# Ten expert tiles turned on VectorE and through DRAM, nine row buffers, and one early table of expert biases

## What is computed

```python
x = x + tanh(g_xattn) * attention(layernorm(x), ctx_1024, ...)   # 8 batches of 512 rows of 512
# the experts, over all 4096 rows at once:
xt = layernorm(x).reshape(4096, 512)
probs = softmax(xt @ router_w + router_b)
gate, idx = max(probs), argmax(probs)                  # one of 8 experts for each row
e_out = xt @ expert_w[idx] + expert_b[idx]
x = x + tanh(g_ffn) * gate * e_out
```

## Time and profile before

| | before |
|---|---|
| median of three runs | 1065.18 us (1064.52 to 1066.03) |
| the profiled execution | 1071.23 us, span of the trace 1069.5 us |
| TensorE busy, share of the span | 1057.6 us, 99% |
| TensorE weight loads | 864.1 us, 81% |
| VectorE busy | 790.9 us, 74% |
| ScalarE busy | 431.9 us, 40% |
| GpSimd busy | 214.8 us, 20% |
| DMA | 146.03 MB, mean 137 GB/s |

### The profile page before, as it was taken

The page is one execution under the profiler, slowest core; times in us unless marked ns, Lnnn a source line. Parts: engine busy times, 40 slices in busy tenths (PEclk is TensorE's granted clock), DMA queues, the critical chain, the costliest instruction groups (busy, mean ns, idle before and its releaser), DMA issues.

```text
span 1069.5 us, 16036 instructions
## 1 busy us (share of the span) xinstructions
PE 1057.6 (99%) x5119; PEld 864.1 (81%) x5119; DVE 790.9 (74%) x1634; ACT 431.9 (40%) x768; POOL 214.8 (20%) x319
## 2 busy tenths in 40 slices
PE   9999999999999999999999999999999999998998
PEld 7878887888788888888888888887888787886886
DVE  6886976777767876677768677866687677976665
ACT  6334623352325242533344234423352346532432
POOL 3000101130113001400140013101220112256664
PEclk9999999999999999999999999999999999998999
DMA  8337416431643254334354335325531754585542
GB/s 300 134 109 226 161 22 174 138 125 39 141 143 112 99 119 124 124 127 99 109 160 128 80 116 171 128 56 140 171 99 24 205 180 146 185 284 180 158 153 75
DMA packets 135468, 146.03 MB, mean 137 GB/s; under 512 B 25242, under 2 KB 87222, under 8 KB 135288
## 3 DMA queue, kind: packets, MB, share of 16 engines
q1 hardware_dynamic: 125248, 119.60, 38.3%
q0 software_dynamic: 7264, 19.20, 5.6%
q10 hardware_dynamic: 2904, 6.63, 1.8%
HBM read 101.30 MB, written 45.93 MB: 138 GB/s over the span
## 4 chain that ended last, share of the span: by engine, by line
PE 89%; DVE 4%; DMA 3%; issue 2%; SPq 1%; ACT 1%; another core or an unknown queue 0%; POOL 0%; DVEq 0%; ACTq 0%; POOLq 0%
PE mm L168 60%; PE u L1145 15%; PE u L168 9%; PE tr L168 2%; PE mm L2027 1%; DVE arena L1382 1%; DMA in_tile<-in_ctx 1%; DMA probs_by_keys<-pairs_as_f 1%; PE tr L1199 1%; DMA slot_as_f<-in_L_xattn_Wk_s 1%; DMA x_rows_early<-slot_as_f 0%; DMA slot_as_f<-in_x_by_blocks 0%; SPq L897 0%; PE tr L1189 0%; ACT probs L1259 0%
## 5 line engine op out<-in xcount | busy, mean ns | idle before, releaser
L168 PE MATMUL mm<-arena 128*128 128x512 f32 x1512 | 356.1, 390 | 0.8 <-DVE arena L1382 0.6
L168 PEld LDWEIGHTS mm<-arena 128*128 128x128 f32 x1512 | 282.5, 188 | 64.6 <-ACT probs L1259 4.1
L168 PE MATMUL mm<-arena,q_pair 128*128 128x512 f32 x768 | 184.1, 394 | 0.0
L1145 PE MATMUL u<-arena 128*128 128x512 f32 x768 | 182.9, 390 | 0.7 <-DVE arena L1382 0.7
L1145 PEld LDWEIGHTS u<-arena 128*128 128x128 f32 x768 | 143.4, 188 | 31.0 <-DVE arena L1382 1.5
L168 PEld LDWEIGHTS mm<-arena,q_pair 128*128 128x128 f32 x768 | 142.0, 188 | 29.4 <-issue 0.5
L1607 POOL TENSOR_SCALAR stats<-stats 128x1 f32<-128x1 f32 x28 | 11.3, 405 | 545.6 <-DVE stats L1521 545.0
L1259 ACT ACTIVATE probs<-mm,neg_top 128x512 f32<-128x512 f32 x64 | 44.2, 690 | 147.9 <-DVE neg_top L1405 147.9
L1252 ACT ACTIVATE arena<-mm 128x512 fp32r<-128x512 f32 x64 | 38.3, 598 | 136.0 <-PE mm L168 121.8
L1382 DVE TENSOR_TENSOR arena<-mm,arena 128x512 fp32r<-128x512 f32 x65 | 44.5, 684 | 65.8 <-ACT arena L1252 39.7
L168 PE MATMUL mm<-q_pair,arena 128*128 128x512 f32 x360 | 86.3, 389 | 0.0
(11 more groups left out here) (281 smaller groups left out, 1441.3 us busy)
## 6 DMA issues: line engine op xcount, KB each, us to landing
slot_as_f<-in_ctx_by_columns SPq DMA_DIRECT2D x8, 1024.0 KB
probs_by_keys<-slot_as_f SPq DMA_DIRECT2D x32, 256.0 KB, 4.1
pairs_as_f<-probs_by_keys SPq DMA_DIRECT2D x8, 1024.0 KB, 5.5
probs_by_keys<-pairs_as_f SPq DMA_DIRECT2D x32, 256.0 KB, 4.5
probs<-probs_by_keys SPq DMA_DIRECT2D x8, 1024.0 KB, 5.6
in_tile<-in_ctx SPq DMA_DIRECT2D x31, 256.0 KB
in_tile<-in_x SPq DMA_DIRECT2D x28, 256.0 KB
slot_as_f<-in_x_by_columns SPq DMA_DIRECT2D x7, 1024.0 KB, 7.0
```

Of the source, the lines that this page charges most:

```text
L168: last = pe.matmul(bank, lhsT(a, c), rhs(b, c), start=start and n == 0, stop=stop and n == C * len(PASSES) - 1)
L1145: last = pe.matmul(u_bank[m][:], v_pair[:, i % 2, a, tile(m)], pt_pair[:, i % 2, p], start=i == 0 and n == 0, stop=i == T - 1 and n == 2)
```

## The change

- Tiles 15, 17, 23, 25, and so on to 37 (TURNED) are no longer transposed by TensorE. ScalarE normalises such a tile in stage n - 6. VectorE transposes its 32 x 32 blocks in stage n - 5, SyncE stores the result to DRAM and in stage n - 4 loads it again in four parts that put the blocks in their places. `high` and `low` in stage n - 1 read the landed tile from SBUF.
- So that both ways give the same order of columns, ScalarE writes the normalised rows of the other tiles in a block order, and the expert weights are given in that order.
- There are nine row buffers from tile 12 on, and the step in which each row is gathered is given by `step_of_gather`.
- The table of all expert biases is loaded once, before T 0, to where the attention's first pair lay, and all tiles read it. The loads of single biases are gone.
- Rows 3, 4 and 5 are gathered when the gate is done (3 and 4 came earlier), and all four residual chunks are loaded then (the first came earlier).
- From T 1 on the steps of the last batch stand one T later in the list.
- Outputs have six buffers, and the wait for a free one stands in `add_bias`.

```diff
-ROWS, NORMED, PAIR, BIAS, BANK, OUT = 6, 3, 3, 5, 4, 5
-FROM_SLOT = 4
-BY_TABLE, LOAD_TABLE = 12, 6
+ROWS, PAIR, BANK, OUT = 9, 3, 4, 6
+SIX_ROWS = 12
+TURNED = (15, 17) + tuple(range(23, TILES, 2))
...
+    turned_dram = [nc.dram_tensor(f"turned_rows{i}", (P, H), F32, kind="Internal").ap() for i in range(2)]
...
-    s += steps("GC2") + load(22, 23) + steps("GC3") + load(24, 25, 26, 27) + steps("EL7") + gather(3, 4)
-    s += steps("RP0 GS0 TN0 XR0 GS1 TP0") + load(28, 29, 30, 31)
+    s += steps("GC2") + load(22, 23) + steps("GC3") + load(24, 25, 26, 27) + steps("EL7")
+    s += steps("RP0 GS0 TN0 GS1 TP0") + load(28, 29, 30, 31)
...
-    names = """GA5 T0 XR1 XR2 XR3 T1 M0 M1 MX0 MX1 BS0 T2 M2 M3 MX2 MX3 BS1 T3 LG0 LG1 BS2 T4 LG2 LG3 BS3 LR3 T5 RT0 IW0
-               T6 RK0 T7 RS0 TB3 T8 RS1 TB4 T9 RS2 T10 RS3 TB5 T11 TB6 T12 T13 LI0 T14"""
+    names = """GA3 GA4 GA5 T0 XR0 XR1 T1 XR2 XR3 T2 M0 M1 MX0 MX1 BS0 T3 M2 M3 MX2 MX3 BS1 T4 LG0 LG1 BS2 T5 LG2 LG3 BS3
+               LR3 T6 RT0 IW0 T7 RK0 T8 RS0 TB3 T9 RS1 TB4 T10 RS2 T11 RS3 TB5 T12 TB6 T13 LI0 T14"""
...
-        sp.wait_ge(x1_stats, 4 * (B - 1))
-        load_last_residual(0)
         for n in range(EARLY // LOADS):
             experts_run("IX", n)
+        sp.wait_ge(gc_mm, 1)
+        for of_last in range(E - 1, E + 1):
+            sp.wait_ge(ex_loaded[of_last], 16)
         experts_run("BIAS", 0)
         sp.wait_ge(g_mm, 4 * B)
-        for c in range(1, C):
+        for c in range(C):
             load_last_residual(c)
...
+    row = [k.in_tile[:, n] for n in range(3)] + [q[:, 4 * H + n * ROWX:4 * H + (n + 1) * ROWX] for n in range(3)]
+    table = c2s.rearrange("p (e d) -> p e d", e=E)
+    row += [slot[:, n * ROWX:(n + 1) * ROWX] for n in range(3)]
+    stage, landed = slot[:, 5 * H:6 * H], [slot[:, n * H:(n + 1) * H] for n in (6, 7)]
+
+    def row_no(n):
+        return n % 6 if n < SIX_ROWS else (n - SIX_ROWS + 6) % ROWS
...
             elif kind == "BIAS":
-                sp.wait_ge(experts_ready, 1)
-                load_bias(0)
+                sp.dma_start(c2s, expert_b.rearrange("e d -> (e d)").partition_broadcast(P)).then_inc(table_loaded, 16)
             elif kind == "T":
...
+                if i + 5 in TURNED:
+                    m = turned_no(i + 5)
+                    sp.wait_ge(turned, probs_turned_in_all + m + 1)
+                    sp.dma_start(turned_dram[m % 2], stage).then_inc(turned_kept, 16)
+                if i + 4 in TURNED:
+                    m = turned_no(i + 4)
+                    sp.wait_ge(turned_kept, turned_kept_in_all + 16 * (m + 1))
+                    if m > 1:
+                        sp.wait_ge(e_lo, TURNED[m - 2] + 1)
+                    if m > 0:
+                        sp.wait_ge(e_hi, TURNED[m - 1] + 1)
+                    for r in range(T):
+                        rows_of_chunk = turned_dram[m % 2].rearrange("(t i) (r n) -> r i t n", i=32, r=T)[r]
+                        sp.dma_start(landed[m % 2][32 * r:32 * r + 32].rearrange("i (t n) -> i t n", t=T),
+                                     rows_of_chunk).then_inc(e_landed, 16)
+                if FIRST_LATE <= i:
+                    for n in range(EARLY + LOADS + 2 * (i - FIRST_LATE), min(EARLY + LOADS + 2 * (i - FIRST_LATE) + 2, TILES)):
+                        load_idx(n)
...
             elif n == 3:
-                pool.wait_ge(attention.gc_mm, 1)
-            elif n == 5:
                 pool.wait_ge(attention.g_mm, 4 * B)
...
+        def step_of_gather(n):
+
+            if n < SIX_ROWS:
+                return n - 5
+            return max(n - 8, 15 + (n - EARLY) // 2) if n >= EARLY else max(n - 8, SIX_ROWS - 5)
...
             elif kind == "T":
-                if ROWS <= i + ROWS - 1 < TILES and i > 0:
-                    gather(i + ROWS - 1)
+                for n in range(6, TILES):
+                    if i == step_of_gather(n):
+                        gather(n)
                 scatter(i)
...
                 if i + 1 < TILES:
                     high(i + 1)
-                if i + 2 < TILES:
+                if i + 2 in by_pe:
                     normalise(i + 2)
+                if i + 6 in TURNED:
+                    normalise(i + 6)
...
+        def turn(n):
+            m = turned_no(n)
+            dve.wait_ge(e_normed, normed_in_order.index(n) + 1)
+            if m > 0:
+                dve.wait_ge(turned_kept, turned_kept_in_all + 16 * m)
+            dve.transpose(stage.rearrange("p (c j) -> p c j", j=32),
+                          normed_of(n).rearrange("p (c j) -> p c j", j=32)).then_inc(turned, 1)
...
                     low(i + 1)
                 add_bias(i)
+                if i + 5 in TURNED:
+                    turn(i + 5)
                 finish(i)
...
-                if i + 1 < TILES:
+                if i + 1 in by_pe:
                     transpose_rows(i + 1)
```

More of the change, by code:

```diff
@@ L607, in attention_part @@
     probs = sb("probs", [P, T, L])
+    with nc.sbuf_tensor("first_pair", [P, 2, C, P], F32R) as first_pair:
+        pass
     normed = sb("normed", [P, H])
@@ L1732, in experts_part @@
[L1732 to L1748, removed]
+    n_pair = [[attention.first_pair[:, a] for a in (HI, LO)]] + [[pair_in(attention.q_pair, n)[:, a] for a in (HI, LO)] for n in range(2)]
@@ new lines, in row_no, with users_of_row, row_is_loaded, turned_no @@
+    def row_no(n):
+        return n % 6 if n < SIX_ROWS else (n - SIX_ROWS + 6) % ROWS
+    def users_of_row(n):
+        return [m for m in range(n) if row_no(m) == row_no(n)]
+    def row_is_loaded(engine, n):
+        engine.wait_ge(row_loaded[row_no(n)], 16 * (len(users_of_row(n)) + 1))
+    def turned_no(n):
+        return TURNED.index(n)
+    by_pe = [n for n in range(TILES) if n not in TURNED]
+    normed_in_order = []
+    for i in range(-2, TILES):
+        if i + 2 in by_pe:
+            normed_in_order.append(i + 2)
+        if i + 6 in TURNED:
+            normed_in_order.append(i + 6)
@@ L1749, in experts_part, with normed_of, tr_bank_of, by_chunks @@
+    def normed_of(n):
+        return normed[2] if n in TURNED else normed[by_pe.index(n) % 2]
+    def tr_bank_of(n):
+        return tr_bank[by_pe.index(n) % 2]
+    def by_chunks(n):
+        if n in TURNED:
+            return landed[turned_no(n) % 2].rearrange("p (t c j) -> p c t j", t=T, c=C)
+        return tr_bank_of(n)[:].rearrange("p (c t j) -> p c t j", c=C, t=T)
+    def half_of(n, a):
+        return n_pair[n % PAIR][a].rearrange("p c (t j) -> p c t j", t=T)
     tr_bank, y_bank = attention.mm_bank, attention.u_bank
@@ L1870, in normalise, with high @@
         def normalise(n):
+            if n == TURNED[0]:
+                act.wait_ge(attention.mix_done, 4 * B - 1)
+            if n in TURNED:
+                if n == TURNED[0]:
+                    act.wait_ge(e_tr, by_pe.index(2) + 1)
+                else:
+                    act.wait_ge(turned, probs_turned_in_all + turned_no(n))
+            elif by_pe.index(n) > 1:
+                act.wait_ge(e_tr, by_pe.index(n) - 1)
+            row_is_loaded(act, n)
+            rows = row[row_no(n)]
+            of, to = rows[:, 0:H], normed_of(n)
+            if n not in TURNED:
+                of, to = of.rearrange("p (r c j) -> p r c j", r=T, c=C), to.rearrange("p (c r j) -> p r c j", r=T, c=C)
+            act.activation(to, of, ACT.Identity, bias=rows[:, H + 1:H + 2], scale=rows[:, H + 2:H + 3]).then_inc(e_normed, 1)
+        def high(n):
+            if n in TURNED:
+                act.wait_ge(e_landed, 16 * T * (turned_no(n) + 1))
+            else:
+                act.wait_ge(e_tr, by_pe.index(n) + 1)
             if n == 0:
[L1873 to L1874 removed]
+                act.wait_ge(attention.mix_done, 4 * B - 3)
+            elif n == 1:
                 act.wait_ge(attention.g_mm, 4 * B)
[L1876 to L1886 removed]
+            act.activation(half_of(n, HI), by_chunks(n), ACT.Copy).then_inc(e_hi, 1)
         def run(kind, i):
@@ L2020, in transpose_rows @@
         def transpose_rows(n):
-            pe.wait_ge(e_normed, n + 1)
+            pe.wait_ge(e_normed, normed_in_order.index(n) + 1)
             if n < 2:
@@ L2024, in transpose_rows @@
             else:
-                pe.wait_ge(e_lo, n - 1)
+                pe.wait_ge(e_lo, by_pe[by_pe.index(n) - 2] + 1)
             for c in range(C):
-                last = pe.transpose(tr_bank[n % 2][:, c * P:(c + 1) * P], normed[n % NORMED][:, c * P:(c + 1) * P],
+                last = pe.transpose(tr_bank_of(n)[:, c * P:(c + 1) * P], normed_of(n)[:, c * P:(c + 1) * P],
                                     ident[:])
```

136 lines of the change are left out of this document (48 added, 88 removed).

## The result

The changed kernel takes 1072.2 us (median, 1070.8 to 1074.2) where the kernel before takes 1065.3: ratio 1.0061, 95% interval [1.0045, 1.0076]. It is slower, by 6.9 us, where 3.3 were forecast. A second run of the pair gave 1072.7 against 1065.9, 1.0068 [1.0051, 1.0085]. The profiled execution took 1071.57 us.

The account below looks back on a forecast made before the run. TensorE, busy for 99% of the span, was taken as the bound. Tile 20's start +4.2, eight transpose groups -3.5 and the clock +2.6 made +3.3: 1065.18 becomes 1068.5 us, range 1060.5 to 1071.5.

Parts of the forecast that it names:

- the sum: Whole kernel: tile 20's start +4.2, eight transpose groups -3.5 and the clock +2.6, together +3.3 us.
- Tile 20's start: Before tile 20's transposes: ScalarE waits for row 23, TensorE stands 5.8 us; start 999.2 against 995.0, +4.2.
- the count of seventeen: GpSimd's queue from scatter 6 to the last list scatter: seventeen instructions at 1.29 each, 21.9 us, ending at 978.6.
- Eight groups: Tiles 23 to 37, behind T(18): eight transpose groups leave TensorE, -3.5 us.
- the clock: After the wait before tile 20: TensorE's granted clock falls, slowing its next work, +2.6 us.
- The round trip: Turned tiles' transpose, store, loads and split: 13.4 us within five stages of 14.9, 1.5 us over; cost nothing.
- rival D: Tail: the round trip is late too, TensorE waits before each turned product, 3.3 + 3 to 6, 1073; chance 0.10.
- Tile 17: SyncE's queue: turned loads of tile 17 end by about 980 and do not hold the first late index load.
- Table, residuals, row 3: Start of the experts' part: early table and loads cost between nothing and +2 us; taken as nothing.
- The hole: Between T(11) and T(12) in the earlier profile: 6.65 us lost, taken as that profiled execution's alone.

Follow-up runs that it names:

- before_again: The kernel before, unchanged, run and profiled again in a quiet batch: 1065.5 us.
- after: The changed kernel in its first profile, against the kernel before: median 1072.2 us, ratio 1.0061; profiled execution 1071.57 us.
- spread_2: Repetition in another quiet batch: changed kernel with no turned tile and gathers from tile 12 on in stage n-5; 0.9992 of the kernel before.
- one_a_stage: Changed kernel with only 25 to 37 turned, turned tiles' gathers in stage n-7, others in n-5; 1.0057 of the kernel before, quiet batch.
- no15_17: Changed kernel with tiles 15 and 17 transposed by TensorE again, 23 to 37 still turned; late-signal batches only: 1.0072, 1.0065 and 1.0065 of the kernel before.
- no23: Changed kernel with tile 23 transposed by TensorE again, 15, 17 and 25 to 37 still turned; late-signal batches only: 1.0115, 1.0097, 1.0087 of the kernel before.
- best: Changed kernel with 15 and 17 unturned, turned tiles' gathers in stage n-8, others in n-5, lists earlier; late-signal batch: 1.0036 of the kernel before.
- spread: Changed kernel with no turned tile and every gather from tile 12 on in stage n-5; quiet batch: 1064.7 us, 0.9990 of the kernel before.
- after_3: The changed kernel, unchanged, in a late-signal batch: 1080.1 us, 1.0088 of the kernel before.
- after_again: The changed kernel, unchanged, run and profiled again in a quiet batch: 1072.7 us.
- best_2: Quiet repetition: changed kernel, 15 and 17 unturned, turned tiles' gathers in stage n-8, others in n-5, lists earlier; 0.9991 of the kernel before.

## Why the forecast was right in kind and short in size

Profiled executions of the quiet kind, before_again beside after:

```
             T(12)    T(18)    T(19)    T(38)    full time
before_again 973.36   992.58   995.77   1056.30  1065.13
after        972.54   993.71   1002.17  1061.50  1071.57
difference   -0.82    +1.13    +6.40    +5.20    +6.44
```

The median moved by 6.9 where the sum said 3.3. Of the 3.6 that are missing, the start of tile 20 has 1.9 to 2.3 and the time outside the span 1.2. Term by term:

- **Tile 20's start, +4.2 forecast, +6.1 to +6.5 measured: the step that failed.** It starts at 1001.54, against 995.42 in before_again and my 995.0. The mechanism and the count of seventeen (the old order, counted alike, has twelve) held; the sizes along the chain did not. Scatter 6 starts at 957.98, not 956.7 (+1.3): GpSimd's four small operations and gather 11 stand ahead of the scatter in the new order and end at 957.68, and I had followed VectorE alone. VectorE's sum was not early either: it waited for T(6)'s product and ended at 956.79, where the forecast needed 955.84. Seventeen instructions took 22.6, not 21.9 (+0.7). From last list scatter to first index load 4.2, not 3.65 (+0.5). Loads to gather 20 5.87, and 20 to 23 5.17, as said. Gather 23 to its use 3.69, not 3.3 (+0.4). From there to TensorE 2.05, not 2.5 (-0.45). Together +2.3, as the forecast's legs were rounded up by some 0.15. The largest part is the start of scatter 6. SyncE was as said not held by tile 17's loads, but they ended at 983.19, not 980.
- **Eight groups, -3.5, and the clock, +2.6.** From T(19) to T(38): 60.53 before, 59.33 after, -1.2. Eight groups are -3.5; T(19) to T(20) took 4.57 instead of 3.21, +1.4 by the clock (granted 0.62 over 1001 to 1004 and 0.72 over 1004 to 1006, then 1.00); waits of 0.22, 0.17 and 0.30 before transposes in the tail, +0.7: together -1.4. With 0.3 more for the slower transposes of tile 20 the clock cost 1.7, less than the forecast 2.6, which was also 0.2 too high by its rows (it holds T(12)'s 4.94 from the timeline against 2.77 from the chain; the timeline has 3.02), and the small tail waits, which I had at nothing, took it back.
- **The round trip, at nothing with 1.5 us to spare, had no spare.** In the changed kernel's tail ScalarE waits for landed tiles too (rival D's sign), up to 2.98 us, and two of TensorE's three small waits (0.22, 0.17) come right behind such a wait; the third (0.30) comes behind 2.54 us for a gathered row. The longest, for tile 27:

```profile
1026.33 0.63 ACT L1916 ACTIVATE first_pair<-slot_as_f 128x512 fp32r<-128x512 f32 x1 [2.98 <-DMA slot_as_f<-turned_rows]
```

  VectorE's transpose of tile 27 ends at 1015.68, 2.9 us into T(22) as forecast. The store goes out only at 1017.17, since SyncE's loads of tile 25 and an index load stand before it; from there to the landing it takes the forecast 9.2. So D's mechanism is there, at 0.4 us where D had 3 to 6.
- **Tile 17, at nothing, was a second place of the same wait.** Normalising 17 stands in stage 11, its gather was issued at 970.22, and ScalarE stood 3.30 (its rows above). TensorE lost 0.72, and 1.65 more since VectorE was late too: its turning, its sums and seven small operations of the late table fell together (0.5 of it is there in spread_2 and one_a_stage too, which turn no tile at that place). T(18) came at 993.71 instead of the forecast 990.65. By the trace it did not set the end, because GpSimd went on without waiting from scatter 6 to 982 and row 23 was late anyway. In the late-signal batch with both, no15_17 took 1077.9 and the changed kernel 1080.1, so there the two tiles cost 2 us, of which the median time outside the span has 0.1. In a quiet batch it was not run.
- **Table, residuals, row 3, at nothing.** 0.57 before tile 3's transposes (0.32 in the second trace), and a gain from T(9) to T(12) of about 1.5 where I took 0.5: the kernel before waits 1.25 there for row 11 (its rows above). Over T(12) the kernel was 0.8 ahead.
- **Around the products.** From T(38) to the full time 10.07 against 8.83: 1.2 us that I did not forecast. It lies outside the span (2.97 against 1.73), in the four runs of the result 2.0 to 3.7. The runs narrow it down: the kernels that turn 15 and 17 (the changed one and no23, 28 runs) have 1.8 to 4.7, every other variant 1.7 to 2.0, best with eight turned tiles 1.8. So it comes with turning 15 and 17; why stays open.
- **The hole.** I took it for the profiled execution's alone. It is a late signal: ScalarE's "remote" in the earlier trace rows is the mark. In the five batches it came in all of a batch's kernels or in none; that first profile (1071.23) is not one of the three runs that were timed for the kernel before (1064.5 to 1066.0), and beside what it was taken is not on record. Its size was 6.4 rather than 6.65: I had set a start of the timeline, 969.85, against one of the chain, 982.90, which the timeline has at 982.66. For the sum this made no difference; for the range it did, since under late signals the same change costs 9 us.

The Trainium skill (DMA: Bandwidth & Descriptors, section Anatomy of one DMA) led to an estimate of 2.6 for the gather's flight. Measured from 1000 to 1060 are 3.2 to 4.4 in spread and its repetition (medians 3.4 and 3.5) and 3.5 to 5.2 in the changed kernel (median 4.1). The traces don't agree with the rule here, and by it the forecast would have been worse.

Neither of the two versions without the stall beats the kernel before by more than 0.1%: spread lies at 0.9990 and 0.9992, best at 0.9991, and of the three intervals only the first ends below 1, at 0.9998.

## What to carry to other kernels

Work taken from the bounding engine may come back as lead time: an operation moved ahead in an in-order queue waits for data that is needed five stages later, and holds up what is needed next. So date the input of every moved operation by its whole chain, through every queue in its new order, and again at each place where the operation recurs. And before an experiment is believed, look whether the kernel before took the time beside it that it took before.

## What the hardware showed

- TensorE's signals can be late. In three batches of five ScalarE started mostly 2 to 5 us after the transposes that it waited for had ended (1.6 to 8.1 over all), four to eight times in the trace of each kernel beside the one before; the kernel before then took 1071 instead of 1065.5, and its first trace, of 1071.2, has one such start (4.5 us). One chip had a batch with and one without. The three batches had four kernels beside the one before, the two others three; whether that matters was not tried.
- An unbroken string of indirect DMAs from GpSimd is not enough to bring them about. In after_3 the first three of the five late starts do fall in or just behind such strings, with pauses of 0.3 us (956.5 to 967.1, 8 of them, and 969.6 to 984.3, 11). But in quiet batches after_again has 20 in a row from 955.6 to 982.0 and best_2 27 from 960.2 to 996.1, with pauses of 0.3 and no late signal. Nor does best, with fewer gathers ahead, lose less: from its quiet batch to the late-signal one it goes from 1064.2 to 1074.2, 10.0 us, the changed kernel from 1072.7 to 1080.1, 7.4 (its quiet batch ran on another chip), and the kernel before, on the chip of best, from 1065.2 to 1071.1. The cause stays open; spread, which would test the gathers' places, met no late-signal batch.
- With half a MB more per pair of tiles in the tail (best_2 against spread_2) the DMA share was 0.76 instead of 0.49 and a gather landed in 3.9 us instead of 3.5 (medians).
